# One gather in twelve of the third and fourth edge pass replaced by one-hot products with a table held in SBUF

## The reference

```python
x = _layernorm(x + _L0_gnn_ref(x, edge_index, edge_attr, ...))   # attention with exp weights
x = _layernorm(x + _L1_gnn_ref(x, edge_index, ...))              # mean and max of neighbours, batch norm
x = _layernorm(x + _L2_gnn_ref(x, weight, bias, src, dst))       # h = x @ W scaled by degrees, sum over edges
x = _layernorm(x + _L3_gnn_ref(x, edge_index, edge_weight, ...)) # below

h = x @ W
msgs = h[src] * edge_weight[:, None]
agg = jax.ops.segment_sum(msgs, dst, num_segments=x.shape[0])
y = agg + bias                                                   # then norm, gamma, beta
```

## Time and profile before

| | us |
|---|---|
| median of 3 runs | 4429.07 |
| lowest, highest | 4424.14, 4434.93 |
| the profiled execution | 4435.99 |
| its span, first to last instruction | 4434.2 |
| mean granted TensorE clock in it | 0.662 of full speed |

### The profile page before, as it was taken

How to read it: one execution, slowest core, us unless ns; L and a number is a source line. 1 busy time by engine, 2 the same in 40 slices (tenths; PEclk the granted TensorE clock), 3 DMA queues, 4 the chain that set the end, 5 groups by cost and what they waited for, 6 DMA issues and landing times.

```text
span 4434.2 us, 55777 instructions
## 1 busy us (share of the span) xinstructions
PE 2574.0 (58%) x15042; PEld 2300.1 (52%) x15042; DVE 1983.8 (45%) x4498; ACT 1374.5 (31%) x4318; POOL 3217.5 (73%) x3366
## 2 busy tenths in 40 slices
PE   7677777777576667677746643333454333333335
PEld 7677777777566666666624433333343333333334
DVE  4666666667576666666661111111123222222225
ACT  2222222223444444444543322222222222222223
POOL 5677777777377777777757777777776777777776
PEclk7877777777688888888965555555555555555555
DMA  7766766766433333333311111111122111111112
GB/s 222 200 183 183 183 183 183 183 184 174 104 100 99 100 99 100 100 98 99 99 37 40 40 40 39 40 40 40 40 47 48 40 39 40 40 39 39 39 40 55
DMA packets 337348, 409.88 MB, mean 92 GB/s; under 512 B 212224, under 2 KB 248691, under 8 KB 336957
## 3 DMA queue, kind: packets, MB, share of 16 engines
q0 software_dynamic: 133120, 245.58, 22.7%
q1 hardware_dynamic: 203933, 160.75, 13.5%
HBM read 386.26 MB, written 19.77 MB: 92 GB/s over the span
## 4 chain that ended last, share of the span: by engine, by line
POOL 49%; issue 24%; PE 14%; DVE 6%; DMA 4%; ACT 1%; SPq 1%; ACTq 0%; DVEq 0%; POOLq 0%
POOL rows L563 48%; PE bank L661 9%; DVE same L1263 3%; DMA rows<-kv_table,src_idx 2%; PE bank L853 1%; DMA rows<-pair_table,src_idx 1%; POOL acc_max L590 1%; SPq L401 0%; PE bank L674 0%; PE bank L706 0%; DVE prod L1332 0%; DVE score L1334 0%; PE bank L675 0%; DVE prod L1330 0%; PE bank L758 0%
## 5 line engine op out<-in xcount | busy, mean ns | idle before, releaser
L661 PE MATMUL bank<-same,rows 128*96 128x128 f32 x4992 | 1088.0, 390 | 1125.8 <-issue 1046.3
L661 PEld LDWEIGHTS bank<-same,rows 128*96 128x96 f32 x4992 | 927.8, 248 | 1257.3 <-issue 1251.8
L563 POOL DMA_INDIRECT rows<-kv_table,src_idx x832 | 795.9, 957 | 312.3 <-issue 272.7
L563 POOL DMA_INDIRECT rows<-pair_table,src_idx x832 | 790.1, 950 | 310.8 <-issue 250.1
L945 ACT COPY acc<-bank 96x511 f32 (+1 forms) x832 | 481.1, 578 | 1655.0 <-PE bank L661 1653.6
L563 POOL DMA_INDIRECT rows<-h_table,src_idx x832 | 793.8, 954 | 271.9 <-issue 253.1
L563 POOL DMA_INDIRECT rows<-ci_table,src_idx x832 | 786.9, 946 | 261.7 <-issue 253.1
L1263 DVE TENSOR_TENSOR same<-bank,rank_col 128x512 f32<-128x512 f32 x624 | 423.4, 679 | 844.6 <-PE bank L661 844.5
L1564 DVE TENSOR_SCALAR same<-iota_s,rank_col,src_hi 128x128 f32<-128x128 f32 x832 | 232.8, 345 | 764.6 <-PE bank L661 764.5
L661 PE MATMUL bank<-same,msg 128*105 128x128 f32 x1664 | 309.0, 345 | 220.4 <-ACT acc L947 220.1
L674 PE MATMUL bank<-weights,first_only 97*128 97x96 f32 x1664 | 397.7, 329 | 29.5 <-DMA first_only<-q_table 26.0
(11 more groups left out here) (168 smaller groups left out, 2946.0 us busy)
## 6 DMA issues: line engine op xcount, KB each, us to landing
first_only<-in_attr_cols SPq DMA_DIRECT2D x104, 384.0 KB, 4.1
first_only<-q_table SPq DMA_DIRECT2D x832, 48.0 KB
first_only<-rank_rows SPq DMA_DIRECT2D x104, 256.0 KB
first_only<-keep_rows SPq DMA_DIRECT2D x104, 192.0 KB
rows<-kv_table,src_idx POOLq DMA_INDIRECT x832
rows<-pair_table,src_idx POOLq DMA_INDIRECT x832
rows<-ci_table,src_idx POOLq DMA_INDIRECT x832
rows<-h_table,src_idx POOLq DMA_INDIRECT x832
```

The costliest lines, as they stand in the source:

```text
L563: pool.indirect_dma_start(rows[:, k, j, 0:width], None, table, bass.IndirectOffsetOnAxis(ap=src_idx[:, t:t + 1], axis=0)).then_inc(rows_in ...
L661: mm = pe.matmul(out[0:nrow, here], left(j), right(j), start=(j == 0), stop=(j == TQ - 1), skip_group_check=True)
```

## The change

Every third quad from quad 18 to quad 195 is "picked": 60 quads in each of the two passes. A picked quad gathers three tiles. The rows of its fourth tile are made by TensorE: a one-hot matrix `found` (49 node tiles of 128 x 128, bf16) marks for each edge its source node, and 49 products with the node table sum into bank[0] what is the row of each source. The table is kept in SBUF as three bf16 parts side by side (288 columns) whose sum is the fp32 value exactly; VectorE adds the three parts while it copies bank[0] to `rows`.

- **Table.** SP loads the table chunk by chunk (13 loads a pass), and VectorE splits each in four instructions (`make_exact`) in the quads 1 to 13 of the pass. The part `near` lies in unused words of `acc_max`, the rest in new words of the carved tile `first_only`.
- **Source rows.** For each picked quad SP loads the 128 source numbers, broadcast to all partitions (`load_sources`). VectorE subtracts the partition's number (`away`, in bank 7).
- **`find`** on VectorE makes `found` in three pieces of 16, 16 and 17 node tiles, in the three quads before the picked one. **`fetch`** on TensorE makes the products of a piece in the same quad, behind the quad's `spread`. **`take`** on VectorE reduces bank[0] into `rows` at the picked quad.
- SP, GpSimd and the first two passes change in nothing else; the counts of the waits for rows follow the smaller number of gathers (`arrivals`).

```diff
+    EVERY = 3
+    PARTS = 3
+    START = NC + 2 + EVERY
+    picked = list(range(START, TAIL * GQ, EVERY))
+    piece_of = [NT * m // EVERY for m in range(EVERY + 1)]
+    order_of = {q: g for g, q in enumerate(picked)}
...
+    def gathers(n, q):
+
+        return TQ - 1 if n > 1 and q in order_of else TQ
...
+            def load_stage(n, c):
+                wait(sp, staged, (n - 2) * NC + c - 1)
+                m = len(tiles_of(c))
+                sp.dma_start(stage[:, c % 2, 0:m, :], rows_of(ci_table if n == 2 else h_table, c, 0, F)).then_inc(stage_in[c % 2].sem, 16)
+
+            def load_sources(n, g):
+                wait(sp, away_done, (n - 2) * len(picked) + g - 1)
+                t = picked[g] * TQ + TQ - 1
+                sp.dma_start(src_row[:, g % 2, :], a["src_rows"][t:t + 1, :].to_broadcast([P, P])).then_inc(src_in[g % 2].sem, 16)
...
-                for j in range(TQ):
+                for j in range(gathers(n, q)):
...
                 wait(pe, s.same_done, q + 1)
-                wait(pe, rows_in[k], s.rows + (i + 1) * 16 * TQ)
+                wait(pe, rows_in[k], arrivals(s.n, q))
+                if q in order_of:
+                    wait(pe, fetched, s.picks + order_of[q] + 1)
                 wait(pe, s.copied, q - 1)
...
+            def fetch(s, q):
...
+                wait(pe, found_done, (s.picks + g) * EVERY + m + 1)
+                for t in range(piece_of[m], piece_of[m + 1]):
+                    mm = pe.matmul(bank[0][:, 0:PARTS * F], found[:, t, :], exact(t)[:, 0, :], start=(t == 0), stop=(t == NT - 1),
+                                   skip_group_check=True)
+                mm.then_inc(found_used.sem, 1)
...
                     spread(s3, q, i, k, places[k])
+                    fetch(s3, q)
...
+            def make_exact(s, c):
...
+                st.did(dve.tensor_copy(part[0], x))
+                st.settle()
+                st.did(dve.tensor_tensor(left[:, 0:n, :], x, part[0], ALU.subtract))
+                st.settle()
+                dve.sem_inc(staged.sem, 1)
+                st.did(dve.tensor_copy(part[1], left[:, 0:n, :]))
+                st.settle()
+                st.did(dve.tensor_tensor(part[2], left[:, 0:n, :], part[1], ALU.subtract))
+                st.settle()
+
+            def find(s, q):
...
+                if m == 0:
+                    wait(dve, src_in[g % 2], ((s.n - 2) * len(range(g % 2, len(picked), 2)) + g // 2 + 1) * 16)
+                    st.did(dve.tensor_scalar(away, src_row[:, g % 2, :], iota_col[:, 0:1], None, ALU.subtract))
+                    st.settle()
+                    dve.sem_inc(away_done.sem, 1)
+                lo, hi = piece_of[m], piece_of[m + 1]
+                wait(dve, found_used, (s.picks + g - 1) * EVERY + m + 1)
+                dve.tensor_tensor(found[:, lo:hi, :], away.rearrange("p (o e) -> p o e", o=1).to_broadcast([P, hi - lo, P]),
+                                  over(hundreds[:, lo:hi], P), ALU.is_equal).then_inc(found_done.sem, 1)
+
+            def take(s, q, k):
+
+                n = s.picks + order_of[q]
+                wait(dve, found_used, (n + 1) * EVERY)
+                dve.tensor_reduce(rows[:, k, TQ - 1, 0:F], bank[0][:, 0:PARTS * F].rearrange("p (m f) -> p f m", m=PARTS), AX_X,
+                                  ALU.add).then_inc(fetched.sem, 1)
...
                     one_hot(same[:, k % 2], iota_over, rank_col, q, P).then_inc(s2.same_done.sem, 1)
+                    if q in order_of:
+                        take(s2, q, k)
+                    if 0 < q <= NC:
+                        make_exact(s2, q - 1)
+                    find(s2, q)
...
                     ins.then_inc(s3.same_done.sem, 1)
+                    if q in order_of:
+                        take(s3, q, k)
+                    if 0 < q <= NC:
+                        make_exact(s3, q - 1)
+                    find(s3, q)
```

More of the change, by code:

```diff
@@ L109, in gnn_kernel, with piece, arrivals @@
     assert TAIL > 14
+    EVERY = 3
[4 more added lines that the diff above has]
+    order_of = {q: g for g, q in enumerate(picked)}
+    def piece(q):
+        for m in range(EVERY):
+            g = order_of.get(q + EVERY - m)
+            if g is not None:
+                return g, m
+        return None
+    def gathers(n, q):
+        return TQ - 1 if n > 1 and q in order_of else TQ
+    def arrivals(n, q):
+        return 16 * sum(gathers(m, p) for m in range(n + 1) for p in range(q % GQ, q + 1 if m == n else NQ, GQ))
     def ripe(slot, lag):
@@ L292, in __init__ @@
                 self.same_done, self.agg_done, self.held, self.copied = (Signal(x, n * NQ) for x in edge_sems)
-                self.rows = n * NG * 16 * TQ
+                self.n = n
+                self.picks = (n - 2) * len(picked)
         passes = [Pass(n) for n in range(4)]
@@ L544, in _, with load_table @@
             sp.dma_start(weight_col[:], a["weight_cols"]).then_inc(s_weight, 16)
+            def load_stage(n, c):
[6 more added lines that the diff above has]
+                sp.dma_start(src_row[:, g % 2, :], a["src_rows"][t:t + 1, :].to_broadcast([P, P])).then_inc(src_in[g % 2].sem, 16)
+            def load_table(n, outs):
+                for b in range(2):
+                    wait(sp, outs[b], 16 * len(range(b, NC, 2)))
+                for c in range(NC):
+                    load_stage(n, c)
+                for g in range(len(picked)):
+                    load_sources(n, g)
+            load_table(2, c_outs)
             for slot in range(NQ + 2):
@@ L553, in _, with edge_pass_pool @@
                 wait(sp, e_outs[b], 16 * len(range(b, NC, 2)))
-        def edge_pass_pool(pool, table, width, freed):
+        def edge_pass_pool(pool, n, table, width, freed):
             for q in range(NQ):
@@ L754, in turn_rows @@
             def turn_rows(q, i, k):
-                wait(pe, rows_in[k], s1.rows + (i + 1) * 16 * TQ)
+                wait(pe, rows_in[k], arrivals(1, q))
                 wait(pe, scan_done, q - 1)
@@ L859, in _ @@
             pe.wait_ge(ones_row, 1)
+            wait(pe, c_act, NC)
             def third_pass(i, kind):
@@ L885, in _ @@
             pe.wait_ge(ones_row, 2)
+            wait(pe, d_sum, NC)
             def fourth_pass(i, kind):
@@ L1472, in _ @@
             s2 = passes[2]
+            def make_exact(s, c):
+                n = len(tiles_of(c))
+                x = stage[:, c % 2, 0:n, :]
+                part = [exact(c * CT, n)[:, :, m * F:(m + 1) * F] for m in range(PARTS)]
+                wait(dve, stage_in[c % 2], ((s.n - 2) * len(range(c % 2, NC, 2)) + c // 2 + 1) * 16)
+                st.did(dve.tensor_copy(part[0], x))
[8 more added lines that the diff above has]
+            def find(s, q):
+                at = piece(q)
+                if at is None:
+                    return
+                g, m = at
+                if m == 0:
[12 more added lines that the diff above has]
+                                  ALU.add).then_inc(fetched.sem, 1)
+            st.did(dve.tensor_scalar(hundreds, iota_s[:, 0:NT], float(P), None, ALU.mult))
+            st.settle()
             dve.memset(x_two_t[F:F1, :, :], 1.0).then_inc(ones_row, 1)
```

35 lines of the change are left out of this document (30 added, 5 removed).

## The result

The changed kernel takes 4280.93 us in the median of 4 runs (4278.2 to 4282.51), the kernel before, over 4 runs, 4432.0. The ratio is 0.9656, with a 95% interval of 0.9644 to 0.9668: 151 us less.

A forecast was written before the change was run, and what follows sets the result against it. The prediction took GpSimd's gather issue to bound the last two passes: 4435.99 profiled - 150.6 for saved gathers + 3 for slower ones = 4288, or 4281 us against the median (4429.1 - 147.6); range 4268 to 4352.

The forecast's parts named there:

- The bound and the 150.6 us: Third and fourth pass: they last as long as GpSimd's gathers take to issue; 60 fewer in each save 150.6 us.
- Products: TensorE's 49 bf16 products of 288 columns: 127 ns each, between 120 and 159, with weight loads hidden; 6.2 us in all.
- rival 3: TensorE's weight load isn't hidden before a bf16 product, 225 ns each; group 16.3 us, 4579 us; chance 0.03.
- The sum of 7.7 and 3.3 us: VectorE's work per three quads, fourth pass: 7.7 us for `find`, `take` and subtraction, besides one-hots at 1.11 us a quad.
- The chain: VectorE and TensorE per three-quad group: 11.5 us in the third pass, 13.2 in the fourth, below gathers of 13.76 and 13.85.
- rival 1: A chain sets the period for part of the passes; group 14.4 us, 4351 us, span 4300 to 4420; chance 0.13.
- The clock: TensorE in the changed passes: mean clock 0.85 or more instead of half, since falling behind means work without a pause.
- gathers beside a busier VectorE: Gathers slow down beside VectorE's new work: 0 to 6.4 us for the third pass, 3 us taken, by the second pass.

The follow-up runs named there:

- all the work with all the gathers: The changed kernel's new work, but every tile gathered too (832 a pass), product sums to a scratch tile; undisturbed 4437.42 us, ratio 1.0006 to the kernel before.
- the doubled products: The changed kernel with every bf16 product made twice, the second into bank[1], which nobody reads; undisturbed 4691.63 us, ratio 1.0591 to the kernel before.
- the undisturbed runs: Second and third series, without the engine stops of the first; the kernel before took 4437.25 and 4431.05 us in them.
- every second quad in the first order: The changed kernel with every second quad picked instead of every third, `take` still before `find`; undisturbed 4896.35 us, ratio 1.1036 to the kernel before.

## Why the prediction was right

**The bound and the 150.6 us** held. Gathers 120 fewer, 151 us less in the medians; all the work with all the gathers costs 0.06%, which is zero within its interval.

**Products.** 127 ns taken between 120 and 159; measured 123. That weight loads are hidden was read from the four short products and is what the longer ones do. The load's median is 98 ns here too, and adding it would give 225 ns; the products follow at 123, so rival 3 is out. The Trainium skill ("TensorE: Matmul & The Clock Gate", part 3, "The mechanism") says that a load overlaps a running product only when the row groups differ. By that sentence the trace disagrees; but the same section also lets a load run ahead when it goes to a background weight buffer, which the prediction passed over and which the trace doesn't contradict.

**VectorE.** `find` 2.29 us (2.26 predicted) and 2.41 (2.39), `take` 0.457 (0.45), the subtraction 0.344 (at most 0.345). The table's four instructions take 1.9 us from 2309.76 us on (2.2 predicted). In 600 us of the fourth pass VectorE is busy 465.7 us, 78%. The sum of 7.7 and 3.3 us in 13.85 was 79%.

**The chain.** Its parts and the standstill of TensorE are in the group shown. That it was 11.5 us in a period of 13.76 isn't to be seen in the change itself, where the margin hides it, but in the doubled products: the same sum gave 17.1 and the trace 17.17. That sum already had the measured 122 ns a product and 0.3 us for the handoffs; with the prediction's 127 ns and 0.5 us it would be 17.7. The margin cost nothing in the undisturbed runs: rival 1 didn't occur. One reading was wrong without effect: SP's loads don't run free in the passes, they wait for VectorE (`staged`, `away_done`), 1682 us of the queue's time from 2300 to 4200 us.

**The clock.** 0.85 or more was forecast, 0.91 to 0.95 came. The reason given, that a TensorE that falls behind works without pause and so comes back to full clock, fits the doubled products, at 1.00 with TensorE 88% busy. It has an exception that the prediction missed: with every second quad in the first order, the regular pause of 2.48 us left the clock at 0.90.

**Mis-sized: gathers beside a busier VectorE.** I put 3 us on it. From start to start it is 1.2498 and 1.2533 us against 1.2507 and 1.2590, which reads as 5 us less in all. But the second pass, whose code is the same, also went from 1.2546 to 1.2516 us: 3.0 ns are a difference between the two executions. Beyond that the third pass is 2.1 ns slower and the fourth 2.7 ns faster, together 0.5 us, nothing. The step took the second pass as the model of a busy VectorE, but what matters is the kind of instruction and not the load. `find` reads one side from PSUM, and no cost of it can be told: the third pass has 1.2498 to 1.2528 us with it where the gathers bound it, and 1.2484 and 1.2507 without. The fourth pass had its 8.3 ns from the one-hots that read and write SBUF. Why these cost less in the changed kernel (3.5 ns over its third pass) though they are as many isn't settled. It isn't the missing gathers, since with all of them kept it is 4.4 ns. What the traces show is that it goes by where in a gather the one-hots fall: in the kernel before, gathers that have one starting 100 to 200 ns after their own start are 46 ns longer in the mean, and those that have one starting 200 to 300 ns after it aren't longer.

**Luck.** The gain in the medians is 151 us, what the sum gives without this term (150.6), and not 148; the two profiled executions lie 158 us apart because the one before is 4 us above its median and the other 3 us below. That the forecast time was met to the microsecond is chance, since the median of before, over four runs, also lies 3 us higher than the one it started from.

## What to carry to other kernels

If the page shows one engine that only waits for its own pauses, take instructions away from it and pay on the idle ones, whatever those cost in busy time, but sum the new dependency chain first: it, not the busy time, says how far this goes. A result that is taken and an input that is prepared on the same engine should stand in the order input first, with two buffers for the result; here that was worth 614 us at nearly the same work. A chain of 11.5 to 13.5 us beside gathers of 13.8 us was enough in undisturbed runs; where the engines stand still at times, even 15.0 us of gathers wasn't, and the same work cost 1.6%.

## What the runs showed of the hardware

- VectorE instructions between SBUF and SBUF hold GpSimd's indirect DMAs up a little: 8.3 ns for each gather in the kernel before, with four one-hots of 128 columns in four gathers, and nothing once they read PSUM. That is a mean: most gathers aren't touched, and a single one beside the table's instructions took 1.29 us instead of 0.94. The Trainium skill ("SBUF — State Buffer", "SBUF: two separate sides") says that a VectorE operation in a 2-port mode, such as an fp32 copy from SBUF to SBUF, keeps GpSimd from writing descriptors while it lasts. The trace agrees in kind: this gather lost 0.35 us, with two instructions between SBUF and SBUF of 0.56 and 0.36 us beside it. Which of them held it up, and in which mode an instruction ran, no run here shows.
- A product of 288 bf16 columns with a new weight of 128 columns takes 122 to 123 ns in a stream at full clock, 0.42 ns a column, although its weight load is 98 ns long.
- The kernel before took 4431 and 4437 us in two series and 5190 and 5245 us in two others. The kernels traced in those two have the same median length of a gather in the last two passes (944 to 947 ns), and stops in between. What stops the engines is open.
